# Local attention blocks: three changes of order within a tile, and the MLP's first norm moved from the second tile of a half to the first

## The chip, the cores and the metric

The kernel runs on one core of one Trainium2 chip. The metric is the device time of one execution in microseconds (us), smaller is better; three runs of the kernel before gave 3209.75, 3215.48 and 3220.48, with a median of 3215.48. The core has five engines with programs of their own that meet through semaphores: PE (TensorE, matrix products into PSUM), DVE (VectorE), ACT (ScalarE), POOL (GpSimd) and SP (SyncE, which issues DMAs here). Each runs its own program strictly in order, so an instruction that waits holds up everything behind it on its engine.

## What is computed

The reference is a chain of adaptive layer norms, attention and feed-forward layers over 2 batches of 1024 tokens with 128 features. The change lies in one stage, six layers of local attention, each with an MLP behind it:

```python
for i in range(6):
    x = attn_layer(shift_tokens(x), Wqkv[i], q_scale[i], k_scale[i], Wo[i]) + x
    x = ffn_layer(shift_tokens(x), ln_g[i], ln_b[i], W1[i], b1[i], W2[i], b2[i]) + x
```

attn_layer projects to 16 heads of 64, normalises queries and keys to unit length, rotates them by tables of cosines and sines, takes a softmax within windows of 32 tokens over the own and the previous window, applies it to the values and projects back with Wo. ffn_layer is a layer norm, then W1 to two halves of 341, one through a GELU as the gate of the other, then W2.

## The kernel before, in words

All of the change is in local_blocks (from line 895). A *tile* is 128 tokens of one layer; a layer has 16 tiles, 8 per batch, and the 8 tiles of one batch in one layer are called a *half* here. stream (line 1046) writes the order of the halves for every engine alike: step 0 and step 1 of a half, then the MLP of the half before, then a loop of three turns with two steps each. Layers 1 to 4 stand in an outer loop. Each step is software-pipelined over three tiles, told by lags: lag 0 projects queries, keys and values of tile T, squares, normalises and rotates them; lag 1 takes the scores, the softmax and the transposes of the probabilities of tile T-1; lag 2 applies the probabilities of tile T-2 to the values, projects with Wo and adds the result to y, which gives z. So when a half begins, the last tiles of the half before are still in the pipe, and its MLP can only begin behind step 1, when the last z is there. Behind the last half, two more steps drain the pipe.

The MLP works on two groups of 512 columns. The norm of its first group (mean over features on PE, centring on DVE, squares on ACT, variance on PE, root on ACT, inverse on DVE, its spreading over the rows on PE, scaling on DVE, shift on ACT) needs only the first four tiles of the half before, and is woven into a step that gets ahead; in the kernel before that is step 1. The norm of the second group runs inside the MLP. PE's part of a step with ahead is mean (line 1344) in front of the values' projection, variance (L1352) behind it, spread (L1359) behind the output projection; DVE's is centre (L1523) ahead of the row sums, then the projection's addition (L1602, L1603), invert (L1529) and, behind the first of four transposes, scale (L1535); ACT's is norm_start (L1245) ahead of the copies of the values and norm_end (L1250 root with its table load, then a wait for scale, then L1252) behind them, at the end of the step.

ACT's program in a plain step: copy of the old keys (L1261), copies of the transposed queries (L1267), edges (L1272, L1273), squares of queries and keys (L1278, L1280), copies of the transposed keys (L1287), square root of the norms (L1292), out_copy(0), which copies one half of the attention's output from PSUM (L1298), an Exp of one column whose result is unused and which brings the load of the Exp table with it (L1304), out_copy(1), the exponentials (L1310), copies of the values (L1320). DVE's: sums of squares and rotation products of the queries (L1554, L1543, L1550), sums of squares of the keys, row_max (L1569), floor and inverse of the norms (L1572, L1575), the subtraction of the row maximum (L1582), cosine product of the keys, row sums (L1591) and their inverse (L1595), sine product of the keys, the transpose into packed (L1616), four transposes into probsT (L1620), and the projection's addition into z (L1602, L1603). POOL's: part of the transposed probabilities (L1201), sum and unit length of the queries (L1178, L1185), which needs the inverse norms, scaling of the probabilities by the inverse sums in two parts (L1219), sum and unit length of the keys in two halves (L1225, L1229). PE's: transposes of the queries (L1375), projections of queries and keys (L1384), transposes of the keys, the mask and the scores (L1406, L1414), probabilities times values (L1436, L1443) in two halves, projection of the values (L1458), output projection (L1472).

## Time and profile before

| what | value |
|---|---|
| median of three runs | 3215.48 us |
| the profiled execution's own time | 3207.3 us |
| its span | 3205.4 us |
| PE busy, share of the span | 2792.9 us, 87% |
| DVE | 2475.1 us, 77% |
| ACT | 2094.2 us, 65% |
| POOL | 1354.0 us, 42% |
| PE's weight loads (beside its products) | 1700.2 us, 53% |
| PE's granted clock over the span | 0.958 of full speed |

The profile is of one execution. The span is the time from its first to its last instruction; what the execution took beside it is 1.9 us. Busy time counts what an engine computes; waiting for a semaphore is not in it. A row of a timeline gives the start and the duration of one instruction or of a run of like ones, and in brackets how long the engine had been idle before it and which engine's instruction ended that. Lines (L1591) are lines of the kernel before.

### The profile page before, as it was taken

How to read it: one execution, taken by the hardware profiler on the slowest of the kernel's cores; microseconds unless marked ns; L12 is line 12 of the kernel's file. 1: busy time of each engine (PE TensorE's matmuls, PEld its weight loads, DVE VectorE, ACT ScalarE, POOL GpSimd, SP SyncE). 2: the span in 40 equal slices, each digit the busy share in tenths (PEclk: the TensorE clock that was granted, in tenths of full speed). 3: DMA queues.
4: the chain of work that ended last, by engine and by line, in shares of the span. 5: the costliest groups of instructions: out<-in, count | busy, mean ns of one | idle time of the engine just before them, and what ended most of it. 6: DMA issues, size and time to landing. Idle time of an engine off the chain costs nothing. (4 is left out here: it accounts for less than half of the span.)

```text
span 3205.4 us, 72148 instructions
## 1 busy us (share of the span) xinstructions
PE 2792.9 (87%) x27236; PEld 1700.2 (53%) x27244; DVE 2475.1 (77%) x3103; ACT 2094.2 (65%) x3079; POOL 1354.0 (42%) x1211
## 2 busy tenths in 40 slices
PE   5799999997588989898988888888888888789997
PEld 3122222224456555555555555555565656468886
DVE  3899999992389788888888888878888879456664
ACT  2488888884177777787778687878787878311111
POOL 2000000000277675867576667666776767200000
PEclk8799999998599999999999999999999999889998
DMA  3011111110100001000100010001000000000001
GB/s 130 26 28 28 29 28 29 29 24 6 35 30 9 6 16 35 8 7 15 35 7 7 15 35 7 7 15 35 7 7 14 14 8 9 10 19 0 0 0 34
DMA packets 56466, 64.36 MB, mean 20 GB/s; under 512 B 24742, under 2 KB 38964, under 8 KB 55348
## 3 DMA queue, kind: packets, MB, share of 16 engines
q1 hardware_dynamic: 55380, 60.58, 7.0%
q8 instruction: 143, 2.34, 0.3%
q10 hardware_dynamic: 864, 0.79, 0.1%
q14 instruction: 79, 0.65, 0.1%
HBM read 36.69 MB, written 7.34 MB: 14 GB/s over the span
## 5 line engine op out<-in xcount | busy, mean ns | idle before, releaser
L886 DVE TENSOR_REDUCE a_minus_max<-a_ps_max 128x1 f32<-128x1024 f32 x512 | 596.9, 1218 | 59.0 <-PE a_ps_max L811 53.8
L794 ACT ACTIVATE a_expT<-a_ps_scoresT 128x512 f32<-128x512 f32 (+1 forms) x683 | 528.8, 808 | 78.9 <-PE a_ps_scoresT L829 68.2
L1178 POOL TENSOR_TENSOR b_turned_q<-b_rot_q,b_turned_q 128x1024 f32<-128x1024 f32 x96 | 227.1, 2365 | 276.7 <-DVE b_turned_q L1550 276.5
L844 PE MATMUL a_ps_out<-a_expT,v_aug 128*32 128x256 f32 x4096 | 327.9, 392 | 5.5 <-ACT a_outT L781 4.8
L1219 POOL TENSOR_TENSOR b_probs<-b_probs,b_inv_sum 128x512 f32<-128x512 f32 x192 | 197.1, 1047 | 249.2 <-DVE b_inv_sum L1595 249.2
L1620 DVE STREAM_TRANSPOSE b_probsT<-b_probs 32x512 f32<-32x512 f32 x384 | 269.4, 701 | 34.0 <-POOL b_probs L1219 25.0
L765 POOL CAST a_max_hi<-a_minus_max 128x16 bf16<-128x16 f32 x32 | 6.3, 197 | 631.7 <-DVE a_minus_max L886 631.7
L1287 ACT ACTIVATE b_kT<-b_psD 64x512 f32<-64x512 f32 x384 | 226.1, 589 | 64.0 <-PE b_psD L1375 58.9
L829 PE MATMUL a_ps_scoresT<-a_q_op,a_k_op 26*128 26x512 bf16 x1024 | 247.2, 385 | 13.1 <-ACT a_expT L794 4.4
L1225 POOL TENSOR_TENSOR b_turned_k<-b_rot_k,b_turned_k 128x512 f32<-128x512 f32 x192 | 243.3, 1267 | 0.2 <-DVE b_turned_k L1550 0.2
L1375 PE MATMUL b_psD<-ident,b_rot_k 128*128 128x128 f32 x768 | 121.4, 284 | 138.1 <-POOL b_rot_k L1229 138.1
L1458 PE MATMUL b_psD<-b_w_qkv,b_xs 128*128 (+1 forms) x384 | 211.3, 638 | 26.5 <-ACT b_outT L1298 26.5
L811 PE MATMUL a_ps_max<-a_k_op,a_q_op 24*128 24x512 bf16 x1024 | 203.6, 396 | 27.9 <-DMA a_k_op<-terms_k 14.2
L1436 PE MATMUL b_psD<-b_probsT,b_v 128*64 128x128 f32 x3072 | 209.9, 279 | 5.6 <-DVE b_probsT L1620 5.6
L1414 PE MATMUL b_psS<-b_kT,b_qT 128*32 128x128 f32 x6144 | 196.9, 276 | 16.0 <-ACT b_kT L1287 15.4
L1472 PEld LDWEIGHTS b_psS<-b_outT,b_w_o 128*128 128x128 f32 x1536 | 187.3, 193 | 40.6 <-issue 39.7
L1201 POOL TENSOR_TENSOR b_probsT<-b_packed,b_ones 32x512 f32<-32x512 f32 x192 | 200.2, 1043 | 16.3 <-POOL b_rot_k L1229 1.2
L1229 POOL TENSOR_TENSOR b_rot_k<-b_turned_k,b_inv_norm 128x512 f32<-128x512 f32 x192 | 200.1, 1042 | 15.1
L1384 PE MATMUL b_psQ<-b_w_qkv,b_xs 128*128 (+1 forms) x384 | 188.3, 614 | 12.8 <-POOL b_xs L1159 12.8
L1375 PEld LDWEIGHTS b_psD<-ident,b_rot_k 128*128 128x128 f32 x768 | 83.2, 141 | 216.6 <-POOL b_rot_k L1229 208.2
L1185 POOL TENSOR_TENSOR b_rot_q<-b_turned_q,b_inv_norm 128x1024 f32<-128x1024 f32 x96 | 182.6, 1902 | 36.6 <-issue 36.6
L1414 PEld LDWEIGHTS b_psS<-b_kT,b_qT 128*32 128x32 f32 x6144 | 156.9, 110 | 72.5 <-issue 35.8
(296 smaller groups left out, 6077.1 us busy)
## 6 DMA issues: line engine op xcount, KB each, us to landing
b_v_edge<-b_v SPq DMA_DIRECT2D x96, 128.0 KB
b_w_qkv<-L_ffn_Wqkv SPq DMA_DIRECT2D x6, 1536.0 KB
a_q_op<-terms_q SPq DMA_DIRECT2D x128, 48.0 KB
a_k_op<-terms_k SPq DMA_DIRECT2D x128, 48.0 KB
joined<-a_outT SPq DMA_DIRECT2D x256, 16.0 KB
b_w_o<-L_ffn_Wo SPq DMA_DIRECT2D x6, 512.0 KB
a_q_op<-a_max_rows SPq DMA_DIRECT2D x128, 4.0 KB
b_w<-L_ffn_W SPq DMA_DIRECT2D x6, 341.0 KB
```

The costliest lines, as they stand in the source:

```text
L794: act.activation(expT[:, to:to + 512 * size], ps_scoresT[:, at:at + 512 * size], ACT.Exp, scale=SCALE_A).then_inc(exp_ready, 1)
L829: pe.matmul(ps_scoresT[:, 512 * (n % 3):512 * (n % 3) + 512], k_op[slot][lo:lo + ROWS + 2, P * kt:P * kt + P], q_op[slot][lo:lo + ROWS + 2 ...
L844: last_mm = pe.matmul(ps_out[lo:lo + 32, 256 * part:256 * part + 256], v_aug[:, b * T8 + kt, head, :], expT[:, at:at + 256], start=(kt == ...
L886: dve.tensor_reduce(minus_max[p % 2][:, side, 0, qt:qt + 1], ps_max[u % 2][:], AX.X, ALU.max, negate=True).then_inc(max_taken, 1)
L1178: pool.tensor_tensor(turned[:], rot[:], turned[:], ALU.add).then_inc(added, 1)
L1225: pool.tensor_tensor(turned_k[:, heads], rot_k[:, heads], turned_k[:, heads], ALU.add).then_inc(sum_k_ready, 1)
L1287: act.activation(kT[1 - par][rows, 4 * half:4 * half + 4, side, W:W + P], psD[half][rows, :].rearrange("p (a b) -> p a b", b=P), ACT.Copy) ...
L1375: last_mm = pe.transpose(psD[half][:, P * (pair % 4):P * (pair % 4) + P], src[:, 2 * pair:2 * pair + 2, :].rearrange("p a b -> p (a b)"), ...
L1414: last_mm = pe.matmul(psS[W * j:W * j + W, P * pair:P * pair + P].rearrange("p (a b) -> p a b", b=2 * W), qT[:, pair, W * j:W * j + W], kT ...
L1436: pe.matmul(psD[half][rows, at:at + P], v[par][:, DH * head:DH * head + DH], probsT[:, head, :], start=(pair % 4 == 0), stop=False, skip_g ...
L1458: pe.matmul(psD[half][:], xs[par][:], w_qkv[:, ds(w_at + 2 * INNER + 512 * half, 512)], start=True, stop=True).then_inc(v_half, 1)
L1620: dve.transpose(probsT[rows, :, rows], probs[rows, :, 1, :]).then_inc(probsT_ready, 1)
```

## The change

In stream, the argument that asks for the norm ahead goes from step 1 to step 0 of a half, and at the end from the last step to the one before. In ACT's step the unused Exp goes ahead of both copies of the attention's output. In DVE's step the subtraction of the row maximum goes ahead of the floor and the inverse of the norms, and in steps without a norm the projection's addition goes from the end of the step to between the transpose into packed and the four transposes.

```diff
             def half(l, b, first=False):
-                step(l, b, 0, 0, (0,) if first else (0, 1, 2))
                 at = l * TILES + b * T8
                 if first:
+                    step(l, b, 0, 0, (0,))
                     step(l, b, 1, 1, (0, 1))
                 else:
-                    step(l, b, 1, 1, (0, 1, 2), (l - 1 + b, 1 - b, at))
+                    step(l, b, 0, 0, (0, 1, 2), (l - 1 + b, 1 - b, at))
+                    step(l, b, 1, 1, (0, 1, 2))
                 if middle:
                     middle(l, b)
...
-            step(DEPTH, 0, 0, 0, (1, 2))
-            step(DEPTH, 0, 1, 1, (2,), (LAST, 1, DEPTH * TILES))
+            step(DEPTH, 0, 0, 0, (1, 2), (LAST, 1, DEPTH * TILES))
+            step(DEPTH, 0, 1, 1, (2,))
...
+                if 1 in lags:
+
+                    act.activation(unused[:], res["eps"][:, 0:1], ACT.Exp)
                 if 2 in lags:
                     out_copy(0)
-                if 1 in lags:
-
-                    act.activation(unused[:], res["eps"][:, 0:1], ACT.Exp)
-                if 2 in lags:
                     out_copy(1)
...
+                if 1 in lags:
+
+                    dve.wait_ge(max_ready, T)
+                    if 2 in lags:
+                        dve.wait_ge(probsT_ready, 4 * (T - 1))
+                    rows = probs[:].rearrange("p h c k -> p h (c k)")
+                    dve.tensor_tensor(rows, scores, row_max[:].unsqueeze(2).to_broadcast([P, HEADS_B, 2 * W]), ALU.subtract).then_inc(shifted_ready, 1)
                 if 0 in lags:
                     dve.wait_ge(norm_ready, T + 1)
                     dve.tensor_scalar(floored[:], norm[:], NORM_FLOOR, None, ALU.max).then_inc(floored_ready, 1)
                     dve.wait_ge(floored_ready, T + 1)
                     dve.wait_ge(unit_k_ready, 2 * T)
                     dve.reciprocal(inv_norm[:], floored[:]).then_inc(inv_norm_ready, 1)
-                if 1 in lags:
-
-                    dve.wait_ge(max_ready, T)
-                    if 2 in lags:
-                        dve.wait_ge(probsT_ready, 4 * (T - 1))
-                    rows = probs[:].rearrange("p h c k -> p h (c k)")
-                    dve.tensor_tensor(rows, scores, row_max[:].unsqueeze(2).to_broadcast([P, HEADS_B, 2 * W]), ALU.subtract).then_inc(shifted_ready, 1)
-                if 0 in lags:
                     rotary_cos(psK, rot_k, parts_k_ready, kT_half, 2)
...
                     dve.transpose(packed[:], probs[:, :, 0, :]).then_inc(packed_ready, 1)
+                    if 2 in lags and not ahead:
+                        add_projection()
                     dve.wait_ge(probs_ready, 2 * T)
...
                 elif ahead:
                     scale(ahead[0], ahead[1], 0)
-                if 2 in lags and not ahead:
+                elif 2 in lags:
                     add_projection()
```

## Rows read from the trace of the kernel before

**Rows 1.** Busy time by engine in the local blocks (window, length, engines, PE clock).

```profile
876.35:2800.40 1924.05, 1674.76 (x17559) 1116.90 (x17558) 1592.08 (x2016) 1449.26 (x2141) 1289.31 (x1076) 0.99 0.06 15
```

**Rows 2.** Groups by line, 876 to 2743: busy, mean ns, idle before, releaser.

```profile
L1591 DVE TENSOR_REDUCE b_row_sum<-b_probs 128x16 f32<-128x1024 f32 x95 | 115.8, 1219 | 58.0 <-ACT b_probs L1310 58.0
```

**Rows 3.** Timeline of DVE, one tile: start, us, instruction, idle before.

```profile
1303.51 1.22 DVE L1554 TENSOR_REDUCE b_norm<-b_square_q 128x16 f32<-128x1024 f32 x1
...
1309.91 1.16 DVE L1582 TENSOR_TENSOR b_probs<-b_psS,b_row_max 128x1024 f32<-128x1024 f32 x1
...
1312.79 1.22 DVE L1591 TENSOR_REDUCE b_row_sum<-b_probs 128x16 f32<-128x1024 f32 x1 [0.60 <-ACT b_probs L1310]
...
1315.55 0.71 DVE L1616 STREAM_TRANSPOSE b_packed<-b_probs 128x512 f32<-128x512 f32 x1
1316.55 2.90 DVE L1620 STREAM_TRANSPOSE b_probsT<-b_probs 32x512 f32<-32x512 f32 x4 [0.29 <-POOL b_probs L1219]
1319.49 0.28 DVE L1602 TENSOR_TENSOR z<-y,b_psS 64x128 f32 x1
...
1320.11 1.22 DVE L1554 TENSOR_REDUCE b_norm<-b_square_q 128x16 f32<-128x1024 f32 x1
```

**Rows 4.** Timeline of ACT, the same tile, and the next first copy.

```profile
1308.28 0.23 ACT L1292 ACTIVATE b_norm<-b_norm 128x32 f32<-128x32 f32 x1 [0.40 <-DVE b_norm L1554]
1309.22 0.60 ACT L1298 ACTIVATE b_outT<-b_psD 128x512 f32<-128x512 f32 x1 [0.71 <-PE b_psD L1443]
1309.83 1.28 ACT L1304 ACT_TABLE_LOAD   x1
...
1311.23 0.58 ACT L1298 ACTIVATE b_outT<-b_psD 128x512 f32<-128x512 f32 x1
1311.71 1.05 ACT L1310 ACTIVATE b_probs<-b_probs 128x1024 f32<-128x1024 f32 x1
...
1325.81 0.60 ACT L1298 ACTIVATE b_outT<-b_psD 128x512 f32<-128x512 f32 x1 [0.71 <-PE b_psD L1443]
```

**Rows 5.** Timeline of POOL, the same tile.

```profile
1310.12 1.90 POOL L1185 TENSOR_TENSOR b_rot_q<-b_turned_q,b_inv_norm 128x1024 f32<-128x1024 f32 x1 [0.33 <-issue]
1314.46 2.05 POOL L1219 TENSOR_TENSOR b_probs<-b_probs,b_inv_sum 128x512 f32<-128x512 f32 x2 [2.44 <-DVE b_inv_sum L1595]
...
1320.17 1.04 POOL L1229 TENSOR_TENSOR b_rot_k<-b_turned_k,b_inv_norm 128x512 f32<-128x512 f32 x1
```

**Rows 6.** Timeline of PE, the same tile and the next.

```profile
1309.90 0.61 PE L1443 MATMUL b_psD<-b_edgeT,b_v_edge 128*64 128x32 f32 x16
1310.44 1.13 PE L1458 MATMUL b_psD<-b_w_qkv,b_xs 128*128 x2
...
1321.26 0.66 PE L1375 MATMUL b_psD<-ident,b_rot_k 128*128 128x128 f32 x4 [1.69 <-POOL b_rot_k L1229]
```

**Rows 7.** Timeline of DVE, the second tile of a half, with the norm.

```profile
1336.70 1.22 DVE L1554 TENSOR_REDUCE b_norm<-b_square_q 128x16 f32<-128x1024 f32 x1
...
1350.11 0.28 DVE L1602 TENSOR_TENSOR z<-y,b_psS 64x128 f32<-64x128 f32 x1 [1.27 <-PE b_psS L1472]
...
1352.15 0.75 DVE L1535 SCALAR_TENSOR_TENSOR b_scaled<-b_centred,b_vecs,b_psS 128x512 f32<-128x512 f32 x1
```

**Rows 8.** Timeline of PE, the first products of that half's MLP.

```profile
1353.80 1.96 PE L1494 MATMUL b_psQ<-b_xn,b_w 128*128 128x512 f32 x4 [1.68 <-ACT b_xn L1252]
```

**Rows 9.** Timeline of ACT, from the old keys to the query squares of one tile.

```profile
1405.39 0.72 ACT L1261 ACTIVATE b_kT<-b_kT,inner_tile 128x512 f32<-128x512 f32 x1
...
1408.30 1.00 ACT L1278 ACTIVATE b_square_q<-b_psQ 128x1024 f32<-128x1024 f32 x1
```

**Rows 10.** Timeline of PE, the first products of the last MLP.

```profile
2777.84 3.75 PE L1494 MATMUL b_psQ<-b_xn,b_w 128*128 128x512 f32 x4 [1.68 <-ACT b_xn L1252]
```

**Rows 11.** Timeline of PE, behind a jump of the outer loop.

```profile
2109.62 1.75 PE L1375 MATMUL b_psD<-ident,b_rot_q 128*128 128x128 f32 x8 [2.59 <-issue]
2111.16 2.92 PE L1384 MATMUL b_psQ<-b_w_qkv,b_xs 128*128 x4
```

More of the change, by code:

```diff
@@ L1298, in out_copy @@
                     act.activation(outT[:, 4 * half:4 * half + 4, :].rearrange("p a b -> p (a b)"), psD[half][:], ACT.Copy).then_inc(outT_held, 1)
-                if 2 in lags:
-                    out_copy(0)
                 if 1 in lags:
@@ L1305, in step @@
                 if 2 in lags:
+                    out_copy(0)
                     out_copy(1)
@@ L1569, in step @@
                     dve.tensor_reduce(row_max[:], scores, AX.X, ALU.max).then_inc(max_ready, 1)
-                if 0 in lags:
-                    dve.wait_ge(norm_ready, T + 1)
-                    dve.tensor_scalar(floored[:], norm[:], NORM_FLOOR, None, ALU.max).then_inc(floored_ready, 1)
-                    dve.wait_ge(floored_ready, T + 1)
-                    dve.wait_ge(unit_k_ready, 2 * T)
-                    dve.reciprocal(inv_norm[:], floored[:]).then_inc(inv_norm_ready, 1)
                 if 1 in lags:
@@ L1583, in step @@
                 if 0 in lags:
+                    dve.wait_ge(norm_ready, T + 1)
+                    dve.tensor_scalar(floored[:], norm[:], NORM_FLOOR, None, ALU.max).then_inc(floored_ready, 1)
+                    dve.wait_ge(floored_ready, T + 1)
+                    dve.wait_ge(unit_k_ready, 2 * T)
+                    dve.reciprocal(inv_norm[:], floored[:]).then_inc(inv_norm_ready, 1)
                     rotary_cos(psK, rot_k, parts_k_ready, kT_half, 2)
```

## The prediction

> **What bounds the kernel now.** I first read the busy shares over the stage of the local blocks, from the first tile's norm on DVE to the last addition of an MLP: 1924 of the 3205 us, PE busy for 1675, DVE for 1592, ACT for 1449, POOL for 1289, at a granted clock of 0.99 [rows 1]. The change touches this stage alone. No engine is full in it, so the next view is the grouping by line, for what DVE, whose program is reordered, waits for: its row sums wait 58.0 us in 95 tiles for the exponentials on ACT, 0.6 in each [rows 2]. The rest is in the timeline of one tile of the inner loop. Its DVE period is 1320.11 - 1303.51 = 16.60 us, with two waits in it, 0.60 for the exponentials and 0.29 of the last transposes for POOL's probabilities [rows 3]; so DVE alone would need 15.71.
>
> What sets 16.60 is a ring through four engines. ACT copies the first half of the attention's output at 1309.22, then loads the Exp table (1309.83, 1.28 us), runs the dummy of 0.1 or so, copies the second half at 1311.23 and starts the exponentials at 1311.71, done at 1312.76 [rows 4]. DVE's row sums start at 1312.79 [rows 3]. POOL scales the probabilities from 1314.46 and, in its order, rotates both halves of the keys until 1321.21 [rows 5]. PE transposes the last keys at 1321.26 [rows 6], and scores and attention follow without a gap worth naming, up to the next first-half copy at 1325.81 [rows 4]. 1325.81 - 1309.22 = 16.59: the ring is closed, and the table load lies in it. The second half of the attention's output has meanwhile been ready since 1309.90 + 0.61 = 1310.51 [rows 6], and waits for that load.
>
> **The changes of order, in a tile of the inner loop.**
> 1. *The Exp dummy ahead of both copies.* The square root ends at 1308.51 [rows 4]. The load then runs to about 1309.81, the dummy to 1310.0; the first copy starts at about 1309.93 in place of 1309.22, the second when its data is there, 1310.55 in place of 1311.23. The exponentials start at 1311.03 in place of 1311.71: 0.68 us less in the ring, once per tile. The later first copy delays the first half of PE's values, now begun at 1310.44 [rows 6], by about 0.15; the second half comes 0.3 earlier, so nothing is behind it.
> 2. *The subtraction ahead of the floor and the reciprocal.* It must be done before 1311.03, and in the old order would end at 1309.91 + 1.16 = 1311.07 [rows 3]; ahead of the two small operations it ends some 0.5 earlier, so it is off the ring. It pushes the inverse norms back by its 1.16. POOL's query unit, which waits for them (now at 1310.12, 1.90 us [rows 5]), then begins at 1311.3 and ends at 1313.2, still before the probabilities are due at 1313.8. Who waits for the queries is PE's next tile, behind the output projection. Cost nothing; if the unit ended later than 1313.8, all of the excess would be in the ring. As the subtraction reads what the row maximum has just written, DVE may lose a start-up of 0.1 to 0.2 us; I set DVE alone at 15.71 without it and take 15.8 as its likely need.
> 3. *The projection's addition between the two transposes.* Its two instructions (1320.11 - 1319.49 = 0.62 [rows 3]) fill the 0.29 us wait and delay the four transposes by about 0.3, which PE needs only at the next attention, about 4 us later. PE's projection must be done by then: it is issued before the next tile's transposes of queries, and today the addition does not wait.
>
> New period: 16.60 - 0.68 = **15.92**, above DVE's 15.8, so the ring still sets it, with about 0.15 us of waiting for exponentials left. An inner loop has six tiles per half, and there are 12 halves: 72 x 0.68 = 49 us. DVE also gets ahead of PE by what its waits shrink beyond that, about 0.4 us, which a half collects once, when its first tile starts: 12 x 0.4 = 5 us. Bounds per tile: at most 0.89 (both waits gone, DVE alone); at least nothing, if another ring of the old length lies beside this one. I take 0.68 because each step of the ring has a row.
>
> **The norm moved from the second tile to the first.** From the start of a half, the old order has a plain tile of 16.59 and then the second tile with the norm: starting at 1336.70, its addition at 1350.11 (1.27 waited for the projection, which the mean and variance delay on PE), the scaling at 1352.15 for 0.75 [rows 7], then the normalised columns on ACT, which PE's first MLP product waits for and begins at 1353.80 [rows 8]. So the MLP begins 16.59 + 17.10 = 33.69 after the half's start.
>
> New: the same seven insertions (mean, centring, squares, variance, root with its table load, inverse, spread, scaling, shift) stand in the first tile, at nearly the same offsets, about 0.3 earlier as the mean need not wait for the later subtraction. ACT is done with the normalised columns just ahead of that product, 16.95 into the tile (today), and so held until 16.65 (new), waiting for the scaling; queued behind that wait is all of ACT's second tile: the copy of old keys, queries, edges, then the squares. From the start of the old-key copy to the end of the query squares is 1408.30 + 1.00 - 1405.39 = 3.91 [rows 9], with no wait in it, so the second tile starts on DVE at about 16.65 - 0.1 + 3.91 = 20.5, not at 15.9. In a plain tile the addition, now behind the first transpose, ends about 12.9 us in (row sums at 8.8 without their wait, 2.76 to the transpose, 0.6 for it, 0.6 for the addition [rows 3]). The MLP's products wait for that alone, since the normalised columns are long there: 20.5 + 12.9 = 33.4 and a hand-over. **Against 33.69 that is nothing gained but 0.2 us**, 11 x 0.2 = 2: the tile hidden behind the MLP's wait is paid back as ACT's late start. Without the move the new order would begin the MLP at about 15.9 + 16.8 = 32.7, so the move by itself costs some 0.7 us per half. Inside the MLP nothing changes: PE runs through it.
>
> In the kernel's last two steps the move does pay. The final step has no new projection to hide the norm; its chain ends with the MLP's first product at 2777.84 [rows 10]. Moved, the norm sits in the step before, stretches it by about 2 us (as the second tile: scaling done 16.2 in [rows 7] and three of the four transposes, 2.2 [rows 3], to come, 18.4 against 16.6), and the last step goes from the attention through copies, projection and addition straight to the MLP: I count 2772.7, 5 us less.
>
> DMAs: no DMA is added, removed or reordered. SP's program passes the same steps; its waits for weights of the MLP (w_mlp_in) come one tile earlier on PE, DVE and ACT, but those weights are loaded six tiles before.
>
> **Sum.** 49 + 5 + 2 + 5 = 61 us. The profiled execution took 3207.3 us (span 3205.4), so 3146 on its own scale; it lies 8.2 under the median of 3215.48, and on that I forecast **3154 us**.
>
> **A rule against it.** The trace shows the table load as 1.28 us, begun 0.01 after the copy ahead of it, and the second copy starts 0.12 behind its end, with the dummy between [rows 4]: a switch costs what its row shows. The Trainium skill (ScalarE: Activation LUTs, What ACT_TABLE_LOAD costs) adds a drain of about 1.38 us to each load. By that the exponentials would start about 1.38 later than I have them, which is later than now; no drain shows in these rows.
>
> **Rivals.**
> *R1, the clock at the MLP.* In the new second tile PE has finished its projection about 2 us before the addition is done, then stands until the MLP. Today it stands 1.68 there and the first products run at 1.96 for four, the 2.4 GHz level [rows 8]. Behind an idle stretch of 2.59 us (a jump of the outer loop) PE fell to 1.2 GHz, and four products took 2.92 [rows 11]. Two lies between. If it falls every time, the first four products take 3.75, as at the kernel's last MLP [rows 10], in place of 1.96: 1.8 x 11 = 20 us, **3174 us**. For it: nothing else runs on PE there; against it: 1.69 us idle in every tile [rows 6] does no harm.
> *R2, DVE alone sets the tile.* If PE and ACT hand over faster than their rows allow me to assume, the period is 15.7: 0.2 x 72 = 15 us more gained, **3139 us**. Against it: POOL's queue is full from probabilities to keys.
> *R3, another ring holds.* The order gains only half, say because POOL's query unit is late by 0.3 or the scores become the wait: 72 x 0.34 = 24 us less, **3178 us**; with no gain at all from order, about **3208**.
> *R4, slower: the switch behind the square root is dearer.* Place: ACT, every tile, now ahead of both copies. If the engine must first empty behind the root, the first copy slips too. It decides from 0.82 us on (0.68 of gain and 0.14 that the second copy waits anyway). At the price of one more load, 1.28, the exponentials would start 0.46 later than today: 72 x 0.46 = 33 us, with the 0.4 per half lost too, about **3245 us**. Against it: the same load behind the first copy shows none.
> *R5, it doesn't do what it says:* the table choice is made when the program is built; if a copy needed another table, a load would come back. Then the gain from order is gone and the time is R3's 3208, with whose chance I count it; against it, today a copy follows the dummy without a load [rows 4].
>
> **How the numbers follow.** Forecast 0.55, R1 0.17, R2 0.08, R3 0.16 (a quarter of it the case of no gain), R4 0.04. The range runs from R2 to beyond R1 and R3's half: **3138 to 3190**. A measurement of this kernel tells about 0.3% (10 us) from no change. Faster by more: 0.92; within: 0.04; slower: 0.04.
>
> **What would show it.** Right: tile periods of 15.9; the wait of the row sums down from 0.6 to 0.1 or 0.2, the wait of the transposes for POOL gone; the Exp load directly behind the root; the second tile of a half starting about 20.5 after the first, and the MLP's first product about 33.5 after it. Wrong: a period near 16.6 with a wait for inverse norms on POOL; products of the MLP at 1.2 GHz; a second tile that starts before 18.

## The result and the profile after

Four runs of the changed kernel gave 3155.05 to 3167.76 us with a median of **3163.97**; the kernel before, beside it, gave 3212.61. The ratio is 0.9846, 95% interval 0.9829 to 0.9862: 49 us less. Forecast were 3154 in a range of 3138 to 3190, so the sign and the range hold, and of the expected 61 us some 13 are missing.

From the first tile's norm on DVE to the last addition of an MLP, the stage of the local blocks took 1874.55 us in the profiled execution, where it had 1923.32 by the same two instructions (the window of [rows 1] is a little wider): 48.8 less, as the medians say. (This execution began the stage 10 us later, at 886.5, since the stages ahead of it, which the change does not touch, took longer; hence its own 3167.8 us against 3207.3 shows only 39.5.) The busy time over the stage in the changed kernel (columns as in [rows 1]: window, length, PE, its weight loads, DVE, ACT, POOL, then PE's granted clock):

```profile
886.52:2761.07 1874.55, 1656.23 (x17560) 1130.08 (x17558) 1581.09 (x2015) 1442.60 (x2130) 1290.36 (x1076) 0.98 0.06 15
```

Busy time is a little lower, by 18.5 us on PE, 11.0 on DVE and 6.5 on ACT; none of these comes near the 48.8, so most of the gain is in waits. One instruction did go: ACT loads a table 259 times in the stage where it did 270, since the moved root leaves the square root's table in place for the second tile. That earns nothing there: in the half shown below the second tile's square root waits 1.44 us for DVE, longer than a load takes (1.28). And one number got worse: the granted clock fell from 0.99 to 0.98. The grouping by line shows what the row sums still wait for, 22.8 us where the kernel before has 59.9 over the whole stage (58.0 in the shorter window of [rows 2]; now in 83 tiles, 0.2 to 0.3 each but for five of 1.0 to 1.4):

```profile
L1590 DVE TENSOR_REDUCE b_row_sum<-b_probs 128x16 f32<-128x1024 f32 x96 | 117.0, 1219 | 22.8 <-ACT b_probs L1310 22.8
```

Now one tile of the inner loop, first DVE's timeline of the changed kernel (start, duration, instruction, idle before it):

```profile
1302.55 1.22 DVE L1554 TENSOR_REDUCE b_norm<-b_square_q 128x16 f32<-128x1024 f32 x1
...
1308.60 1.23 DVE L1576 TENSOR_TENSOR b_probs<-b_psS,b_row_max 128x1024 f32<-128x1024 f32 x1
...
1311.58 1.22 DVE L1590 TENSOR_REDUCE b_row_sum<-b_probs 128x16 f32<-128x1024 f32 x1 [0.21 <-ACT b_probs L1310]
...
1314.97 0.24 DVE L1601 TENSOR_TENSOR z<-y,b_psS 64x128 f32 x1
1315.23 0.29 DVE L1602 TENSOR_TENSOR z<-y,b_psS 64x128 f32 x1
1315.55 2.90 DVE L1621 STREAM_TRANSPOSE b_probsT<-b_probs 32x512 f32<-32x512 f32 x4
1318.49 1.22 DVE L1554 TENSOR_REDUCE b_norm<-b_square_q 128x16 f32<-128x1024 f32 x1
```

then ACT's in the same tile:

```profile
1307.34 0.23 ACT L1293 ACTIVATE b_norm<-b_norm 128x32 f32<-128x32 f32 x1
1307.58 1.28 ACT L1303 ACT_TABLE_LOAD   x1
1308.88 0.20 ACT L1303 ACTIVATE b_unused<-eps 128x1 f32<-128x1 f32 x1
1309.09 0.60 ACT L1299 ACTIVATE b_outT<-b_psD 128x512 f32<-128x512 f32 x1
1310.01 0.60 ACT L1299 ACTIVATE b_outT<-b_psD 128x512 f32<-128x512 f32 x1 [0.32 <-PE b_psD L1443]
1310.50 1.05 ACT L1310 ACTIVATE b_probs<-b_probs 128x1024 f32<-128x1024 f32 x1
```

1318.49 - 1302.55 = 15.94, forecast 15.92. Every sign announced for the inner loop is in these rows: the load stands directly behind the square root, the second copy waits for PE's data and no longer for the table, the row sums wait 0.21 where they waited 0.60 [rows 3], and the addition fills the place in which the transposes waited for POOL's probabilities; they wait for nothing now.

The second tile of a half of the changed kernel, the one which the norm has left, in ACT's timeline, DVE's and PE's:

```profile
1334.49 0.72 ACT L1253 ACTIVATE b_xn<-b_scaled,b_vecs 128x512 f32<-128x512 f32 x1 [3.38 <-DVE b_scaled L1535]
1335.12 0.71 ACT L1262 ACTIVATE b_kT<-b_kT,inner_tile 128x512 f32<-128x512 f32 x1
...
1338.00 1.00 ACT L1279 ACTIVATE b_square_q<-b_psQ 128x1024 f32<-128x1024 f32 x1
```

```profile
1339.03 1.22 DVE L1554 TENSOR_REDUCE b_norm<-b_square_q 128x16 f32<-128x1024 f32 x1 [2.38 <-ACT b_square_q L1279]
...
1351.41 0.29 DVE L1602 TENSOR_TENSOR z<-y,b_psS 64x128 f32<-64x128 f32 x1
```

```profile
1341.05 1.08 PE L1414 MATMUL b_psS<-b_kT,b_qT 128*32 128x128 f32 x32 [1.77 <-ACT b_kT L1288]
1342.28 1.08 PE L1414 MATMUL b_psS<-b_kT,b_qT 128*32 128x128 f32 x32 [0.15 <-ACT b_kT L1288]
...
1347.92 1.95 PE L1472 MATMUL b_psS<-b_outT,b_w_o 128*128 128x128 f32 x16
1352.22 3.57 PE L1494 MATMUL b_psQ<-b_xn,b_w 128*128 128x512 f32 x4 [2.35 <-issue]
```

ACT stands 3.38 us for the scaling, with the second tile's queries and squares queued behind it; this half began with its first tile at 1318.49, so the second starts 20.54 after it (forecast 20.5), and the MLP's first product 33.73 after it (33.4 and a hand-over, before 33.69). The starts are as counted. The duration in the last row is not: four products take 3.57 us where [rows 8] has 1.96. PE went to 1.2 GHz behind 2.35 us without work: its granted clock is 0.57 of full speed from 1352 to 1356 and 1.00 in the four us before. Products of the MLP at 1.2 GHz were announced as a sign of being wrong, and this one came. The addition ends at 1351.70; the 0.52 us from there to the product is "issue", time in which the profile shows nothing that PE waits for. That PE's program evaluates its waits in it is my reading.

In the half before, it came elsewhere. PE's timeline of that half's second tile:

```profile
1187.06 1.08 PE L1414 MATMUL b_psS<-b_kT,b_qT 128*32 128x128 f32 x32 [1.76 <-ACT b_kT L1288]
1188.30 1.93 PE L1414 MATMUL b_psS<-b_kT,b_qT 128*32 128x128 f32 x32 [0.15 <-ACT b_kT L1288]
1190.16 1.79 PE L1436 MATMUL b_psD<-b_probsT,b_v 128*64 128x128 f32 x16
...
1199.78 1.95 PE L1494 MATMUL b_psQ<-b_xn,b_w 128*128 128x512 f32 x4 [2.36 <-issue]
```

Here the second 32 scores and the first attention products run at half speed (1.93 and 1.79 where 1.08 and 1.09 are usual), behind the new stand of 1.76 us ahead of the scores; the MLP then starts at full speed behind 2.36. Going through all eleven halves with an MLP inside: 5 falls in the second tile, 3 at the MLP, 3 halves without; each costs 1.6 us or so (the MLP start to the next tile's norm is 24.2 to 24.3 in place of 22.63; the second tile's start to the MLP is 14.7 to 14.8 in place of 13.2, and 14.3 in place of 12.7 in the last two halves). That is 8 x 1.6 = 13 us. The kernel before has none at these places in eleven halves; at the jumps of the outer loop its clock falls three times (one is in [rows 11]), where this execution has one such fall.

So the 48.8 us can be divided, by the differences of the two traces between the same instructions:

| stretch | expected | measured |
|---|---|---|
| tiles of the inner loops, 71 periods | -54 (49 and 5) | -51.9 |
| start of a half to its MLP's first product, 11 halves | -2 | +4.7, of which five falls make 8.0 |
| that product to the next tile, 11 halves | 0 | +4.9, three falls |
| the end, up to the last MLP's first product | -5 | -4.4 |
| the last MLP | 0 | -2.2 |
| the first two tiles | 0 | +0.2 |
| sum | -61 | -48.8 |

Without the eight falls it would be -61.7, some of it by luck, as told below. Whether it is the move that makes them, and whether they can be had out, was the question for the runs.

### The profile page after: what moved, and what is told of

It is laid out like the page before. It is cut to its first block and busy times, and to the rows that moved or that the text cites. A ratio compares the mean times of both kernels' runs of the same rounds, so it can differ in the third digit from the quotient of the medians.

```text
span 3165.9 us, 72145 instructions
## 1 busy us (share of the span) xinstructions
PE 2786.2 (88%) x27244; PEld 1715.3 (54%) x27244; DVE 2464.9 (78%) x3103; ACT 2087.8 (66%) x3068; POOL 1355.2 (43%) x1211
## 5 line engine op out<-in xcount | busy, mean ns | idle before, releaser
L844 PE MATMUL a_ps_out<-a_expT,v_aug 128*32 128x256 f32 x4096 | 334.9, 400 | 5.5 <-ACT a_outT L781 4.8
L811 PE MATMUL a_ps_max<-a_k_op,a_q_op 24*128 24x512 bf16 x1024 | 203.6, 396 | 28.0 <-DMA a_k_op<-terms_k 14.3
L1472 PE MATMUL b_psS<-b_outT,b_w_o 128*128 128x128 f32 x1536 | 189.6, 277 | 0.8 <-ACT b_outT L1299 0.8
L1458 PE MATMUL b_psD<-b_w_qkv,b_xs 128*128 (+1 forms) x384 | 189.2, 615 | 0.0
```

The costliest lines, as they stand in the source:

```text
L811: last_mm = pe.matmul(ps_max[u % 2][:, 512 * half:512 * half + 512], q_op[slot][lo:lo + ROWS, P * qt:P * qt + P], k_op[slot][lo:lo + ROWS, ...
L844: last_mm = pe.matmul(ps_out[lo:lo + 32, 256 * part:256 * part + 256], v_aug[:, b * T8 + kt, head, :], expT[:, at:at + 256], start=(kt == ...
L1472: last_mm = pe.matmul(psS[:, 0:P], w_o[:, pair, :], outT[:, pair, :], start=(pair == 0), stop=(pair == PAIRS - 1))
```

## The experiments

Each number of a half below is read from the trace's rows of three instructions: DVE's first norm of a tile (its start), the first MLP product on PE, and DVE's first norm of the tile behind the MLP. "Second tile" is its start after the first tile's, "MLP" the MLP's first product after the half's start, and a half is counted as fallen when the MLP takes 24 or more to the next tile's start, or the second tile is lengthened as above. One execution of each kernel was traced, so a count of falls is that execution's; the times are medians of four to ten.

**1. The order without the move.**

```diff
+                step(l, b, 0, 0, (0,) if first else (0, 1, 2))
...
-                    step(l, b, 0, 0, (0,))
...
-                    step(l, b, 0, 0, (0, 1, 2), (l - 1 + b, 1 - b, at))
-                    step(l, b, 1, 1, (0, 1, 2))
+                    step(l, b, 1, 1, (0, 1, 2), (l - 1 + b, 1 - b, at))
...
-            step(DEPTH, 0, 0, 0, (1, 2), (LAST, 1, DEPTH * TILES))
-            step(DEPTH, 0, 1, 1, (2,))
+            step(DEPTH, 0, 0, 0, (1, 2))
+            step(DEPTH, 0, 1, 1, (2,), (LAST, 1, DEPTH * TILES))
```

> The three changes of order without the move of the norm. Theory A (the ring: the order gives some 0.65 us per tile of the inner loop, the move gives nothing at the start of the MLPs, costs falls of PE's clock in 8 of 11 halves at 1.6 us each, and gives some 4 us at the end of the stage): loop tiles of 15.94 as in the changed kernel, the MLP's first product about 32.7 us after its half's start (33.7 to 35.5 in the changed kernel), no fall of the clock in the second tile or at the MLP; 3164 - 13 - 11 + 4 = about 3145 us. Theory B (the norm in the first tile is what lets the MLP begin without waiting, so it pays): slower than the changed kernel, 3175 us or more.

Measured: 3158.55 us, ratio 0.982 (0.9796 to 0.9845), stage 1875.64. Tile 15.94, second tile 15.94, MLP at 32.7 to 32.8 in most halves: these starts are as expected. But the time is not the 3145 expected and its interval overlaps that of the changed kernel, since 8 of the 11 MLPs fell where I had expected none, behind stretches that in the kernel before bring no fall. PE's timeline at two MLPs of this one execution:

```profile
1046.93 1.16 PE L1358 MATMUL b_psS<-ident,b_inv_sd 128*128 128x128 f32 x8 [0.89 <-DVE b_inv_sd L1528]
1049.77 3.52 PE L1493 MATMUL b_psQ<-b_xn,b_w 128*128 128x512 f32 x4 [1.69 <-ACT b_xn L1252]
...
1353.25 1.16 PE L1358 MATMUL b_psS<-ident,b_inv_sd 128*128 128x128 f32 x8 [0.89 <-DVE b_inv_sd L1528]
1356.09 1.96 PE L1493 MATMUL b_psQ<-b_xn,b_w 128*128 128x512 f32 x4 [1.69 <-ACT b_xn L1252]
```

The idle stretches are equal to 0.01 us, 0.89 and 1.69; one MLP starts at 1.2 GHz and the other at 2.4. So the move's longer stand is not needed for a fall: they come with the order alone too, and the length of the stand does not decide alone.

**2. The order, and the move in the kernel's last two steps only.** As the first, with the last two steps as in the changed kernel.

> The three changes of order, and the move of the norm in the kernel's last two steps alone. Theory A: 4 to 5 us better than the order alone, by the last MLP beginning earlier, so about 3140 us and some 24 us better than the changed kernel. Theory B: as the order alone or slower than the changed kernel.

Measured: 3149.78 us, ratio 0.9797 (0.9771 to 0.9823), stage 1871.91; 9 of 11 MLPs fell. From the last full tile's start to the last MLP's first product it takes 46.15 us, where the order alone has 51.42, the kernel before 51.28 and the changed kernel 46.84. The move at the end gives some 5 us, and the last MLP's first four products run in 1.95 in place of the 3.75 of [rows 10] (below, the same row in the changed kernel). The time is 14 us below the changed kernel's, not the 24 expected, and its interval overlaps that of the order alone; the nine falls, which I had not expected, are worth 14 us at 1.6 each:

```profile
2741.44 1.96 PE L1494 MATMUL b_psQ<-b_xn,b_w 128*128 128x512 f32 x4 [0.72 <-issue]
```

**3. The move without the order** (the kernel before with the norm in step 0).

```diff
-                step(l, b, 0, 0, (0,) if first else (0, 1, 2))
...
+                    step(l, b, 0, 0, (0,))
...
-                    step(l, b, 1, 1, (0, 1, 2), (l - 1 + b, 1 - b, at))
+                    step(l, b, 0, 0, (0, 1, 2), (l - 1 + b, 1 - b, at))
+                    step(l, b, 1, 1, (0, 1, 2))
...
-            step(DEPTH, 0, 0, 0, (1, 2))
-            step(DEPTH, 0, 1, 1, (2,), (LAST, 1, DEPTH * TILES))
+            step(DEPTH, 0, 0, 0, (1, 2), (LAST, 1, DEPTH * TILES))
+            step(DEPTH, 0, 1, 1, (2,))
```

> The move of the norm alone, in the kernel before: none of the three changes of order. Theory A (the move starts the second tile late by ACT's wait, and is only paid back because the addition now stands ahead of the four transposes): second tile about 20.8 us after the first, the MLP's first product about 16.6 behind that, 37.4 us after the half's start against 33.69: 11 x 3.7 = 41 us lost, 4 to 5 gained at the end, falls of the clock on top: 3250 to 3265 us. Theory B (the move by itself lets the MLP begin earlier): under 3210 us.

Measured: 3280.39 us, ratio 1.0202 (1.0176 to 1.0229): **slower** than before by 68 us, and 15 above the expected 3250 to 3265. The second tile starts 20.8 to 21.0 after the first, MLP at 37.6 to 38.2, and all eleven fell, by 1.4 to 3.1 us (24.0 to 25.7 to the next tile's norm). PE's timeline at one of them:

```profile
1057.91 3.75 PE L1495 MATMUL b_psQ<-b_xn,b_w 128*128 128x512 f32 x4 [5.31 <-DVE z L1604]
```

With the addition at the end of the step, behind four transposes of 2.9 us, the MLP waits for it: 5.31. In the changed kernel, where the addition stands ahead of the transposes, PE waits 1.9 to 2.4 there.

**4. The Exp alone, and 5. DVE's two changes alone.** The fourth kernel is before with the dummy Exp ahead of both copies, the fifth before with the subtraction and the addition moved.

```diff
+                if 1 in lags:
+
+                    act.activation(unused[:], res["eps"][:, 0:1], ACT.Exp)
                 if 2 in lags:
                     out_copy(0)
-                if 1 in lags:
-
-                    act.activation(unused[:], res["eps"][:, 0:1], ACT.Exp)
-                if 2 in lags:
                     out_copy(1)
```

> The Exp dummy ahead of both copies, alone, in the kernel before. Theory A (the table load is what the ring gives up): tiles of the inner loop of 15.95 to 16.05 in place of 16.60, DVE's wait for exponentials down to 0.1, that for POOL still 0.29: 72 x 0.6 = 43 us less work in the ring, 3170 to 3180 us with the clock's falls at the MLPs. Rival (the gain needs all three changes, DVE being nearly full): tiles above 16.3, 3190 us or more.

> The subtraction ahead of the floor, and the addition between the transposes, alone; the Exp dummy stays between the two copies. Theory A (neither lies in the ring): tiles of 16.6 still, DVE waiting about 0.9 in one place, the row sums, in place of 0.6 and 0.29; but the MLP begins about 0.3 earlier: 3205 to 3215 us. Rival (DVE's own length sets the tile): tiles of 16.0 or less, 3170 us.

Measured: the Exp alone 3165.41 us, a little under the expected 3170 to 3180, ratio 0.985 (0.9833 to 0.9866), tile 16.0, 6 falls; DVE's two alone 3206.27 us, ratio 0.9974 (0.9956 to 0.9992), tile 16.6, 5 falls. The grouping by line, first of the Exp alone, then of DVE's two alone:

```profile
L1619 DVE STREAM_TRANSPOSE b_probsT<-b_probs 32x512 f32<-32x512 f32 x384 | 269.3, 701 | 33.9 <-POOL b_probs L1219 24.9
L1590 DVE TENSOR_REDUCE b_row_sum<-b_probs 128x16 f32<-128x1024 f32 x96 | 117.0, 1219 | 8.5 <-ACT b_probs L1309 8.3
```

```profile
L1621 DVE STREAM_TRANSPOSE b_probsT<-b_probs 32x512 f32<-32x512 f32 x384 | 269.3, 701 | 11.9 <-POOL b_probs L1219 0.3
L1590 DVE TENSOR_REDUCE b_row_sum<-b_probs 128x16 f32<-128x1024 f32 x96 | 117.1, 1220 | 79.2 <-ACT b_probs L1310 79.2
```

With the Exp ahead, the waits for the exponentials are nearly gone and those for POOL's probabilities (0.29 in a tile, 24.9 in all) are left: 15.71 of DVE alone and 0.29 give the 16.0. With DVE's two alone the opposite: no wait for POOL, but what DVE gains it waits for ACT, 79.2 where the kernel before has 59.9, and the tile keeps its 16.6. The ring decides; DVE's reorder alone earns nothing in a plain tile, and together with the Exp 0.06 more. It does earn 0.4 in the tile behind an MLP: 17.42 before, 17.02 with DVE's two alone, and 16.77 with the Exp alone, which is the ring's 0.65 and no more.

**6. The kernel before, with halves that last longer.** Two row maxima more in the first step of a half, whose results nobody reads; nothing is touched at the MLP.

```diff
+                    if isinstance(s, int) and s == 0 and 2 in lags:
+                        for i in range(2):
+                            dve.tensor_reduce(pause[i][:], scores, AX.X, ALU.max)
```

> The kernel before, with two more row maxima into tiles that nobody reads ahead of the true one in the first step of each half that has one behind it: the half gets about 1.7 us longer and everything behind it comes later by that, with nothing changed at the MLP's start, where PE stands 0.89 and 1.69 us as before. Question: why the order alone shows 8 falls of the clock in 11 MLPs behind the same two idle stretches that brought none in the kernel before. Theory C (it hangs on when in time the stretches fall, and the kernel before had 11 of 11 escape): falls in 3 or more of the 11 MLPs, 3213 + 19 + 5 to 18 = 3237 to 3250 us. Rival (something in the new order, as PE's work ahead of the MLP, brings them): no falls, about 3232 us.

Measured: 3243.64 us, ratio 1.0092 (1.0075 to 1.0109). 10 of the 11 MLPs fell, where the kernel before has none. In five of the halves the clock fell in the second tile as well, each time behind the stand for the last keys, 1.69 as in [rows 6], with 0.5 to 0.6 of idle time just ahead of it (0.85 to 1.0 us longer each; the granted clock is 0.50 from 1356.3 to 1359.7). PE's timeline in the third half, where the 64 scores take 2.46 (2.02 without a fall), then of the first and the eleventh:

```profile
1354.37 0.66 PE L1376 MATMUL b_psD<-ident,b_rot_k 128*128 128x128 f32 x4 [0.61 <-POOL b_rot_k L1230]
1356.71 1.11 PE L1376 MATMUL b_psD<-ident,b_rot_k 128*128 128x128 f32 x4 [1.69 <-POOL b_rot_k L1230]
...
1358.61 2.46 PE L1415 MATMUL b_psS<-b_kT,b_qT 128*32 128x128 f32 x64
```

```profile
1043.37 1.10 PE L1345 MATMUL b_psS<-z,mean_mat 128*128 128x512 f32 x2 [0.76 <-issue]
...
1049.91 1.16 PE L1360 MATMUL b_psS<-ident,b_inv_sd 128*128 128x128 f32 x8 [0.89 <-DVE b_inv_sd L1530]
1052.75 3.53 PE L1495 MATMUL b_psQ<-b_xn,b_w 128*128 128x512 f32 x4 [1.69 <-ACT b_xn L1253]
...
2663.59 1.16 PE L1360 MATMUL b_psS<-ident,b_inv_sd 128*128 128x128 f32 x8 [0.89 <-DVE b_inv_sd L1530]
2666.43 1.95 PE L1495 MATMUL b_psQ<-b_xn,b_w 128*128 128x512 f32 x4 [1.69 <-ACT b_xn L1253]
```

The stretches of 0.89 and 1.69 ahead of the MLP are those of [rows 8] to 0.01 us, and so is the 0.76 ahead of the mean (0.76 to 0.81 in the kernel before); what differs is that the first tile of the half lasts 1.5 longer, with 0.8 us more of small idle stretches on PE (0.28 and 0.51) ahead of the second tile's scores. So the kernel before was not safe at 1.69; in its one trace it escaped eleven times in a row. The first and the eleventh half of this run have the same rows on PE from the second tile's last keys to the MLP, to 0.02 us, and different outcomes. What decides between them was not isolated.

**7. Fillers that keep PE busy.** The changed kernel, with one product of 512 columns ahead of the scores of the second tile and two ahead of the MLP's wait for the addition, none of them read; the waits that come true early are evaluated ahead of them.

```diff
+                        if isinstance(s, int) and s == 1:
+                            pe.matmul(psS[:, 0:512], mean_mat[:], rope_base[:, 0].rearrange("p a b -> p (a b)"), start=True, stop=True)
...
+                pe.wait_ge(square_q_ready, begun)
+                pe.wait_ge(parts_q_ready, 2 * begun)
+                for _ in range(2):
+                    pe.matmul(ps_gate[0], mean_mat[:], w_1[:, 0:512], start=True, stop=True)
                 pe.wait_ge(z_ready, ended)
                 pe.wait_ge(outT_held, 2 * ended)
                 pe.wait_ge(v_held, 2 * begun)
-                pe.wait_ge(square_q_ready, begun)
                 pe.wait_ge(square_k_ready, begun)
-                pe.wait_ge(parts_q_ready, 2 * begun)
                 pe.wait_ge(parts_k_ready, 2 * begun)
```

> The changed kernel with idle stretches of PE filled by products that nobody reads: one of 512 columns ahead of the mask in the second step (overwritten by the mask), two of 512 ahead of the MLP's wait for the last addition (overwritten by the MLP's first product). Theory A (the 8 falls to 1.2 GHz come from PE standing 1.77 and 2.35 us): no falls, no second tile or MLP longer by 1.6 us, about 13 us better, 3151 us. Rival (the falls come from elsewhere, or the fillers delay what counts): 3164 us or more, falls still there.

Measured: 3145.0 us, ratio 0.9786 (0.9763 to 0.9808), stage 1859.24: 15.3 below the changed kernel's. No fall in eleven halves; from the MLP's first product to the next tile it is 22.66 in every one. PE's timeline at one MLP:

```profile
1182.43 1.95 PE L1474 MATMUL b_psS<-b_outT,b_w_o 128*128 128x128 f32 x16
1184.21 1.88 PE L1485 MATMUL b_psQ<-b_w,mean_mat 128*128 128x512 f32 x4
1186.27 1.98 PE L1498 MATMUL b_psQ<-b_xn,b_w 128*128 128x512 f32 x4 [0.17 <-DVE z L1606]
```

The fillers (L1485) lie in the wait for the addition, and the product starts 0.05 after the addition, where it was 0.52 (the 0.17 in its row counts from the end of the fillers); by my reading, since fewer waits are left to evaluate. 13 for the eight falls and 8 x 0.47 = 4 for the hand-over in the halves of the loop, less 2.2 at the end, make the 15: the missing 13 us are the clock. The 2.2 (49.0 from the last full tile to the last MLP, where the changed kernel has 46.8) are some 1.0 for the fillers, which take 1.7 there where PE waited 0.72, and 1.4 for the last projection, which ran at 1.2 GHz in this execution (3.49 in place of 2.05).

**8. The order and the move at the end, with the MLP's fillers** (the second kernel, with the seventh's lines at the MLP).

> The order and the move in the kernel's last two steps alone, plus two filler products of PE ahead of the MLP's wait. My theory: the filler removes the falls of the clock at the MLP (9 of 11 without it, 1.6 us each: 14 us), and because PE then evaluates part of its waits earlier, the first MLP product starts some 0.3 us sooner in the loop. First product 32.3 to 32.8 us after the half's start, all eleven MLPs at 2.4 GHz, stage 1853 to 1857 us, time 3131 to 3137 us. Since the move inside the loop is worth nothing by my theory, this should be below the changed kernel with the same fillers (3145) by 4 to 12 us. Rival, the move inside the loop does pay once the clock is out of the way: not below 3145.

Measured: 3142.62 us, ratio 0.9779 (0.9757 to 0.9802), stage 1858.78; no fall in eleven, MLP at 32.6 to 33.0 but for two of 33.4. The falls are gone as expected (13.1 off the second kernel's stage), but the time is not the 3131 to 3137 expected, and the stage is the seventh kernel's to 0.5 us. Part of the miss is at the end: 50.07 from the last full tile to the last MLP, 3.9 more than the second kernel. PE's timeline there:

```profile
2711.99 3.58 PE L1471 MATMUL b_psS<-b_outT,b_w_o 128*128 128x128 f32 x16 [0.76 <-ACT b_outT L1298]
2715.40 1.88 PE L1482 MATMUL b_psQ<-b_w,mean_mat 128*128 128x512 f32 x4
2717.12 1.88 PE L1495 MATMUL b_psQ<-b_xn,b_w 128*128 128x512 f32 x4
```

At the last MLP there is only 0.72 of waiting to fill and the fillers take 1.7, so they are in the way; and the projection (3.58, in the second kernel 2.05) ran at 1.2 GHz. Another part is the hand-over, which I had expected 0.3 earlier: without the move the MLP waits for the normalised columns and not for PE's program, and the two fillers last as long as that wait, 1.7. The rest is in the first tiles of the stage, which took 1.8 longer than in the second kernel up to the fourth tile. With the clock out of the way, the move inside the loop does not pay: the MLP comes 0.46 later with it (33.2 to 33.4 in kernel 7, 32.7 to 32.95 here, in most halves), 5 us in eleven halves. The two stages are equal all the same, as this execution lost that much at the first tiles, the jumps and the end, and the times, 3145.0 and 3142.6, have overlapping intervals.

**9. ACT's wait moved out of the second tile.** In the changed kernel, ACT's shift of the scaled columns goes to the front of the MLP; PE's scores in the second tile wait for the scaling in its place.

```diff
+            def norm_shift(l, b, n):
+                G = l * GROUPS + 2 * b + n
...
+                norm_shift(l, b, 0)
...
+                        norm_shift(l, b, 1)
...
+                        if isinstance(s, int) and s == 1:
+                            pe.wait_ge(scaled_ready, (l - 1 + b) * GROUPS + 2 * (1 - b) + 1)
```

> The changed kernel, but ACT's last operation of the moved norm (the wait for the scaling and the shift into the normalised columns) goes from the end of the first step to the front of the MLP, so that nothing of ACT's second step stands behind that wait; PE's mask waits for the scaling. Theory A (ACT's wait is what holds the second tile): the second tile starts about 18.2 us after the first, not 20.55, the MLP's first product 31.3 after it; the 1.77 us in which PE stands before the scores of the second tile are gone and with them the falls of the clock there: 11 x 2.4 + 5 x 1.6 = 34 us better, about 3130 us. Rival (DVE or PE, with the norm's extra work in the first tile, holds the second tile anyway): a start above 20 and no change, about 3164 us.

Measured: 3148.67 us, ratio 0.9804 (0.9779 to 0.983), stage 1862.13. The second tile starts 19.0 after the first, not 18.2, the MLP's first product comes at 32.85 in the loop's halves, not at 31.3, no fall is left ahead of the scores (the stand there is 0.90) and 5 of 11 MLPs fell. The gain on the changed kernel is 15 us where I had expected 34. PE's timeline shows what took the wait's place:

```profile
1168.44 1.16 PE L1364 MATMUL b_psS<-ident,b_inv_sd 128*128 128x128 f32 x8 [0.89 <-DVE b_inv_sd L1536]
1169.43 1.04 PE L1380 MATMUL b_psD<-ident,b_rot_q 128*128 128x128 f32 x8
```

PE's spread of the norm stands ahead of the second tile's query transposes, and waits for DVE's inverse, which comes after the projection's addition; the transposes follow it without a gap.

**10. All of it together.** Kernel 9, with the moved norm's root ahead of ACT's value copies, its inverse ahead of DVE's addition, and kernel 7's two fillers at the MLP.

```diff
+                    norm_end(ahead[0], ahead[1], 0)
...
-                if ahead:
-                    norm_end(ahead[0], ahead[1], 0)
...
-                    add_projection()
                     invert(ahead[0], ahead[1], 0)
+                    add_projection()
```

> The changed kernel, with everything of the moved norm taken out of the second tile's way: ACT's normalised columns moved to the front of the MLP, the moved norm's root ahead of the value copies, its inverse ahead of the projection's addition so that PE's spread no longer holds the transposes of queries, and two filler products ahead of the MLP's wait. My theory: what made the move worth nothing is the late second tile (19.0 to 20.5 us after the first); with the root and inverse early it starts 17.8 to 18.3 after, the MLP's first product comes 31.3 to 31.9 after the half's start, without falls of the clock; stage 1840 to 1848 us, time 3122 to 3132 us. Rival, the second tile stays at about 19 because another of the moved norm's seven insertions holds it: first product 32.3 to 32.8, time 3134 to 3140 us.

Measured: **3124.33 us**, ratio 0.9728 (0.9708 to 0.9748), stage 1835.08, some 40 us below the changed kernel in both; the stage is 5 under the expected 1840 to 1848. Second tile 18.0 to 18.3 and MLP at 31.2 to 31.4 in all halves but one, the MLP 0.1 earlier than the expected span, and no fall. PE's timeline:

```profile
1170.54 1.06 PE L1363 MATMUL b_psS<-ident,b_inv_sd 128*128 128x128 f32 x8
1171.43 1.04 PE L1379 MATMUL b_psD<-ident,b_rot_q 128*128 128x128 f32 x8
...
1178.11 1.08 PE L1420 MATMUL b_psS<-b_kT,b_qT 128*32 128x128 f32 x32 [0.90 <-ACT b_kT L1291]
...
1188.81 1.98 PE L1502 MATMUL b_psQ<-b_xn,b_w 128*128 128x512 f32 x4 [0.17 <-DVE z L1610]
```

The spread no longer waits. So the norm in the first tile can pay, once it no longer holds the second tile: 2.0 us per half against kernel 7 (33.27 to 31.24), and 1.55 against kernel 8 (32.79), which has the same fillers at the MLP and no move inside the loop. How much of it the early root and how much the early inverse gives was not separated.

## Why the prediction was right, and where it was off

**Changes of order: right.** The ring was the bound, and the table load in it the piece to take out: period 15.94 against 15.92, and the three parts alone (kernels 4 and 5) give 16.0 and 16.6, as the ring says. In all 51.9 of 54: 46.3 from the ring, where I had 49, and 0.6 at the outer loop's jumps. The other 5.0 are the 12 x 0.4 of the sum, right in size by luck: I had them where a half's first tile starts, as DVE's lead over PE, but that tile gains no more than the others. They come in the tile behind an MLP (17.42 to 16.36), and kernel 5 shows that DVE's two changes bring them with the period still at 16.6. R2 (DVE alone at 15.7) and R3 (another ring) are out. R4 is out by the load's row: 1.28, begun 0.01 behind the root, and the dummy 0.02 behind its end. By the drain of about 1.38 us which the Trainium skill (ScalarE: Activation LUTs, What ACT_TABLE_LOAD costs) adds, the dummy could not have started there; the trace decides against it in this place too. (The time that I gave for R4, 3245, is a slip: 3208 and 33 make 3241.)

**The norm moved: right in its starts.** Second tile 20.54 against 20.5; MLP 33.73 against 33.69 before, so neither gain nor loss at that point, and about 1 us later than the order alone (32.7 to 32.8), where I had 0.7. ACT's wait with a tile queued behind it was the right mechanism, and kernel 9 shows the next one, PE's spread. The end gave 4.4 of the 5 counted (51.28 to 46.84), and 2.2 more that I had not counted, most of it because the last MLP now starts at 2.4 GHz.

**The step that failed** is the one on the clock: "against it: 1.69 us idle in every tile does no harm", by which R1 got 0.17 as something that would happen every time or not at all, and only at the MLP. It happened in 8 of 11 halves of the traced execution for 1.6 each, 13 us; 3 at the MLP, where R1 had it, and 5 behind ACT's late keys in the second tile, a stand of 1.77 which the same working makes visible (squares late by 4.6) and which I did not follow to PE. The row I leaned on still holds for plain tiles, where none of some 60 such stands brought a fall in the changed kernel either. But it was no evidence for the MLP: the 0.89 and 1.69 there brought a fall 0 times in 11 before, 8 times in kernel 1 and 10 in kernel 6, and in kernel 6 the stand of the row itself brought one in 5 of 11 second tiles, with a short idle stretch ahead of it. All else together came out at 61.7 for 61, and that it is so near is luck: the ring gave 2.7 less than counted, the last MLP 2.2 more, and the tiles around the outer loop's jumps, with one fall in place of three, about 2.0 more.

**What stayed open.** What decides whether the clock falls behind a given idle stretch. Also whether the kernel before escapes in each of its executions, and how the number of falls varies between executions; of each kernel only one was traced.

## What to carry to other kernels

When an instruction is hoisted into an earlier tile, list what queues up behind its wait on every engine it touches: here ACT's shift, then PE's spread, each held the next tile until all were moved, and only then did the hoist pay. A wait on PE is worth filling with products that nobody reads, if it is really a wait; where none is (the last MLP), fillers only lengthen the path. And an idle stretch that a profile shows as harmless for PE's clock may be harmless in that one kernel only: here a change of period brought falls behind the same stretches. So price such a change with a fall there too (1.6 us each here), whatever the rows show for it now.

## What the runs showed of the hardware that was not expected

PE's clock fell to 1.2 GHz behind single stretches of 1.76 to 2.35 us without work, and behind 1.69 with a shorter stretch (0.5 to 0.9) a few products earlier, in some cases and not in others of the same length within one execution. Behind the 0.89 and 1.69 ahead of the MLP it fell in 0 of 11 halves in the kernel before, 8 of 11 with the order, 10 of 11 with the longer first tile. During a fall products of 512 columns took 1.06 us each in place of 0.59, about three of them, and the whole cost was 1.6 us; behind 5.3 to 5.7 us without work it was up to 3.1. Products that nobody reads, put into the waits, took the falls at these places away in all eleven halves (kernels 7, 8 and 10). The Trainium skill (TensorE: Matmul & The Clock Gate, A second HAM failure mode: psum-queue depth-cycling) tells of a kernel whose PE idles briefly between groups of products, often enough that the clock goes down and up again and again. These traces agree that short stretches can do it (0.89 and 1.69), with the addition that equal stretches do not always do so.

In the halves of the outer loop PE started the MLP about 0.52 us after the last addition ended (1351.70 to 1352.22), and 0.10 after it in the halves outside, with the same waits in its program. With two of these waits and two fillers ahead of the wait for the addition it is 0.05 in every half (kernels 7 and 10). My reading is that the waits are evaluated one behind another; fillers and waits were not tried apart.
